# Two planes instead of four in a macaron block: pair merging on TensorE, and the shared expert's pieces spread out

## What is computed

```
x = x + 0.5 * ffn(layernorm(x))
x = x + linear_attention(layernorm(x))      # 16 heads, causal, b_qkv and b_out
x = x + 0.5 * ffn(layernorm(x))             # the same weights again

ffn(xf): scores = softmax(xf @ gate_w.T)                       # 64 experts
         idx    = top 6 of (scores + gate_b); weights = scores[idx]
         each expert takes its first CAP = 64 tokens, in token order; the others are dropped
         h = silu(xb @ w1[e].T) * (xb @ w3[e].T);  yb = h @ w2[e].T      # inner size 88
         y[token] += weight * yb
         z = silu(xf @ ws1.T) * (xf @ ws3.T) @ ws2.T                    # shared expert, inner 176
         return y + z
```

## Time and profile before

| | before |
|---|---|
| median of the runs | 537.15 us (536.43 to 538.29) |
| profiled execution | 532.9 us, span 531.2 us |
| mean granted TensorE clock | 0.793 of 2.4 GHz |
| busy, share of the span | PE 67%, PEld 50%, DVE 58%, ACT 39%, POOL 45% |
| HBM read and written | 39.53 MB and 31.46 MB |
| first slot loop and its adds | about 52 to 164 us |
| second slot loop and its adds | about 393 to 500 us |

### The profile page before, as it was taken

How to read it: one execution, slowest core, us unless ns; L and a number is a source line. 1 busy time by engine, 2 the same in 40 slices (tenths; PEclk the granted TensorE clock), 3 DMA queues, 4 the chain that set the end, 5 groups by cost and what they waited for, 6 DMA issues and landing times.

```text
span 531.2 us, 14693 instructions
## 1 busy us (share of the span) xinstructions
PE 356.6 (67%) x5808; PEld 263.3 (50%) x5812; DVE 307.6 (58%) x999; ACT 207.8 (39%) x543; POOL 237.0 (45%) x215
## 2 busy tenths in 40 slices
PE   0874589999960013598999999218848999998000
PEld 0851475666650012376788888118327667666000
DVE  6488363545430994454777775394985544545077
ACT  3983112322310067744677762169722232231000
POOL 7161747887872000403333333001537888887400
PEclk9987567999995556678999999657855699999555
DMA  8999961001015996000111111454200100100396
GB/s 272 369 268 341 318 185 15 5 11 14 5 6 218 407 401 239 2 2 2 40 40 40 40 40 49 109 218 139 61 8 8 12 11 6 17 5 6 108 426 257
DMA packets 49746, 62.64 MB, mean 118 GB/s; under 512 B 21701, under 2 KB 36248, under 8 KB 47183
## 3 DMA queue, kind: packets, MB, share of 16 engines
q1 hardware_dynamic: 37423, 60.51, 33.3%
q0 software_dynamic: 12288, 1.70, 3.2%
HBM read 39.53 MB, written 31.46 MB: 134 GB/s over the span
## 4 chain that ended last, share of the span: by engine, by line
PE 53%; DVE 23%; DMA 9%; ACT 6%; issue 5%; POOL 3%; SPq 1%; POOLq 0%; DVEq 0%; ACTq 0%
PE bank L769 6%; PE upper L864 5%; PE bank L705 5%; DVE X L957 5%; PE bank L718 5%; PE upper L705 4%; DMA Cb<-planes_d 4%; PE upper L778 3%; DVE Cb L1094 3%; DVE bn L962 3%; DVE Cb L1025 3%; POOL planes_d L452 3%; ACT Cb L560 2%; ACT A L508 2%; PE bank L880 2%
## 5 line engine op out<-in xcount | busy, mean ns | idle before, releaser
L452 POOL DMA_INDIRECT planes_d<-Bb,put_i x64 | 101.4, 1584 | 28.0 <-issue 14.8
L480 POOL TENSOR_TENSOR Bb<-Cb,chm 128x576 f32<-128x576 f32 x32 | 36.9, 1183 | 124.3 <-PE upper L909 69.6
L466 POOL DMA_INDIRECT A<-rows_d,tok_i x64 | 68.0, 1063 | 41.6 <-DVE put_i L1066 22.7
L672 PE MATMUL bank<-ident,A 128*128 128x128 f32 x96 | 21.3, 396 | 81.9 <-ACT A L508 65.1
L672 PEld LDWEIGHTS bank<-ident,A 128*128 128x128 f32 x96 | 17.0, 209 | 85.1 <-ACT A L508 52.3
L1106 DVE TENSOR_SCALAR Bb<-upper,A 64x128 f32<-64x128 f32 x128 | 44.4, 347 | 1.3
L1094 DVE TENSOR_TENSOR Cb<-Cb,upper 88x512 f32<-88x512 f32 x24 | 16.4, 683 | 44.8 <-ACT Cb L560 44.8
L769 PEld LDWEIGHTS bank<-ring,w1s 128*88 128x88 f32 x256 | 34.2, 191 | 8.0 <-issue 8.0
L433 POOL TENSOR_TENSOR Bb<-Eb,st 128x512 f32<-128x512 f32 x8 | 8.3, 1043 | 63.8 <-DVE st L1013 63.8
L560 ACT ACTIVATE Cb<-bank 88x512 f32<-88x512 f32 x24 | 14.2, 592 | 55.1 <-PE upper L705 55.1
L769 PE MATMUL bank<-ring,w3s 128*88 128x64 f32 x256 | 35.6, 270 | 0.0
(11 more groups left out here) (162 smaller groups left out, 804.7 us busy)
## 6 DMA issues: line engine op xcount, KB each, us to landing
planes_d<-zeros SPq DMA_DIRECT2D x8, 2048.0 KB, 15.9
rows_d<-A SPq DMA_DIRECT2D x8, 512.0 KB, 6.0
A<-planes_d SPq DMA_DIRECT2D x4, 1024.0 KB, 6.0
PL<-planes_d SPq DMA_DIRECT2D x4, 1024.0 KB, 10.0
Bb<-planes_d SPq DMA_DIRECT2D x4, 1024.0 KB, 13.7
Cb<-planes_d SPq DMA_DIRECT2D x4, 1024.0 KB, 18.0
w1s<-in_w1T SPq DMA_DIRECT2D x4, 704.0 KB
w3s<-in_w3T SPq DMA_DIRECT2D x4, 704.0 KB
```

Of the source, the lines that this page charges most:

```text
L452: pool.indirect_dma_start(out=planes_d[f], in_=Y[:, s, :], in_offset=None, out_offset=bass.IndirectOffsetOnAxis(ap=put_i[:, s:s + 1], axis=0),
L466: pool.indirect_dma_start(out=GAT[:, t % RING, :], out_offset=None, in_=rows_d, in_offset=bass.IndirectOffsetOnAxis(ap=tok_i[:, t:t + 1], ...
L480: pool.tensor_tensor(out=VX[:, :, :, c, :].rearrange("p q h f -> p (q h) f"), in0=VN.rearrange("p q h f -> p (q h) f"), in1=chm[:, c:c + 1 ...
L672: ins = pe.transpose(bank[g % 2][:, (i % 4) * P:(i % 4 + 1) * P], A[:, i, :], ident[:, :])
```

## The change

- Two planes instead of four, one for each slot parity. Where a token of a slot's second expert is also in its first, the second's row is added to the first's on chip: `spread` (DVE) writes the first expert's tokens as a diagonal for eight slots, `token_rows` (PE) turns it into a row on 64 partitions by a matmul with ones, `match` (DVE) compares it with the second expert's tokens. The result `SAME` is a 0/1 matrix of each slot. `merge` (PE) multiplies it with the second half of Y, `add_second` (DVE) adds that to the first half. The index of a merged row is put out of range, so that POOL's DMA leaves it out.
- The turn's order. PE: transpose, expert_out(s - 2), hidden(s - 1), merge(s - 2), then the piece. DVE: weigh, gate, add_second, then the rest. add(s) on POOL now waits for add_second.
- The shared expert's pieces. Groups 4 and 5 have their hidden pieces ahead of the loop; groups 0 to 3 have their pieces in turns 8, 10, ... 30; outputs of 4 and 5 in turns 32 and 33; groups 6 and 7 in turns 34 to 39, behind the loop. SP's read of the planes waits for six shared groups instead of eight; `update` still waits for all eight.
- The table and first comparison ahead. differences(2) and (3), the first token_rows, spread(0), match(0), table(2) and table(3) stand before the loop; the other three spreads and matches in turns 4 to 19.
- The planes are cleared ahead of everything in one go; the loads of experts 16 to 63 wait until the second slot has been transposed.
- The factor 0.5 moves from `weigh` into `update`, whose two adds become scalar_tensor_tensor.

```diff
+    SPREAD, ROW_TURN, MATCH = (4, 12, 18), (5, 13, 19), (6, 13, 19)
+    LOOPED = 4
+    TURNS = NS + 9
-        planes_d = [nc.dram_tensor(f"planes{f}_d", (4 * T, D), ...
+        planes_d = [nc.dram_tensor(f"planes{f}_d", (2 * T, D), ...
+        PLANES = (A_flat[:, 0:HP], A_flat[:, HP:T], PL[:, 0:HP], PL[:, HP:T])
         def shared_part(s):
+            if s < NS:
+                g, k = divmod((s - 8) // 2, 3)
+                return (g, k) if s >= 8 and s % 2 == 0 and g < LOOPED else None
+            if s < NS + EARLY:
+                return LOOPED + s - NS, 2
+            g, k = divmod(s - NS - EARLY, 3)
+            return (LOOPED + EARLY + g, k) if LOOPED + EARLY + g < NSH else None
 # SP
-                    clear_planes(sp, 0, (2, 3))
+                    sp.wait_ge(xbT_ps, 2)
                     for h in range(1, NQT):
                         load_experts(h)
...
-                sp.wait_ge(z_added, NSH * (f + 1))
+                sp.wait_ge(z_added, NSH * f + LOOPED + EARLY)
 # PE
+                def token_rows(h):
+                    pe.wait_ge(rows_set, NQT * f + h + 1)
+                    if NQT * f + h:
+                        pe.wait_ge(same_ready, NQT * f + h)
+                    ss = slice(QSL * h, QSL * h + QSL)
+                    pe.matmul(bank[LOOK[1]][CAP:P, :], ones[:, :], ROWS[:, ss, :].rearrange("p s c -> p (s c)"),
+                              start=True, stop=True).then_inc(rows_ps, 1)
...
+                differences(2)
+                differences(3)
+                token_rows(0)
...
+                def merge(s):
+                    if s % QSL == 0:
+                        pe.wait_ge(same_ready, NQT * f + s // QSL + 1)
+                    pe.wait_ge(weighed, f * NS + s + 1)
+                    pe.matmul(bank[(4, 7)[s % 2]][0:CAP, D:2 * D], SAME[:, s, :], Y[CAP:P, s, :], start=True, stop=True)\
+                        .then_inc(merged, 1)
...
+                for s in range(TURNS):
                     if s < NS:
                         xb_turn(s)
+                    if s == 2:
+                        pe.wait_ge(dr_sb, NQT * (f + 1))
+                    if 2 <= s < NS + 2:
+                        expert_out(s - 2)
                     if 1 <= s <= NS:
                         hidden(s - 1)
-                    if s >= 2:
-                        expert_out(s - 2)
+                    if 2 <= s < NS + 2:
+                        merge(s - 2)
+                    if s in ROW_TURN:
+                        token_rows(1 + ROW_TURN.index(s))
+                    if s < 2:
+                        look_up(2 + s)
 # DVE
                     dve.wait_ge(z_added, NSH * (n // 2 + 1))
-                    for k in range(4):
-                        then(dve.tensor_tensor(xt, xt, PLANES[g]...[:, :, k, :], ALU.add))
+                    for k in range(2):
+                        then(dve.scalar_tensor_tensor(xt, PLANES[g]...[:, :, k, :], 0.5, xt, ALU.mult, ALU.add))
...
+                def spread(h):
+                    ss = slice(QSL * h, QSL * h + QSL)
+                    dve.tensor_tensor(ROWS[:, ss, :], ident[0:CAP, 0:CAP].unsqueeze(1).broadcast_to([CAP, QSL, CAP]),
+                                      sl[0:CAP, 1, ss].unsqueeze(2).broadcast_to([CAP, QSL, CAP]), ALU.mult).then_inc(rows_set, 1)
+
+                def match(h):
+                    ss = slice(QSL * h, QSL * h + QSL)
+                    dve.wait_ge(rows_ps, NQT * f + h + 1)
+                    then(dve.tensor_tensor(SAME[:, ss, :], bank[LOOK[1]][CAP:P, :].rearrange("p (s c) -> p s c", s=QSL),
+                                           sl[CAP:P, 1, ss].unsqueeze(2).broadcast_to([CAP, QSL, CAP]), ALU.is_equal))
+                    then(dve.tensor_reduce(sl[CAP:P, 0, ss], SAME[:, ss, :], AX, ALU.max))
+                    then(dve.scalar_tensor_tensor(sl[CAP:P, 0, ss], sl[CAP:P, 0, ss], float(T), sl[CAP:P, 1, ss], ALU.mult, ALU.add))
+                    dve.scalar_tensor_tensor(put_i[CAP:P, ss], sl[CAP:P, 0, ss], 2.0, plane0[CAP:P, ss], ALU.mult, ALU.add)\
+                        .then_inc(same_ready, 1)
...
+                def add_second(s):
+                    dve.wait_ge(merged, f * NS + s + 1)
+                    dve.tensor_tensor(Y[0:CAP, s, :], bank[(4, 7)[s % 2]][0:CAP, D:2 * D], Y[0:CAP, s, :], ALU.add).then_inc(y_sb, 1)
+
+                for s in range(TURNS + 1):
+                    if 2 <= s < NS + 2:
+                        weigh(s - 2)
                     if 1 <= s <= NS:
                         gate(s - 1)
+                    if 2 <= s < NS + 2:
+                        add_second(s - 2)
+                    if s in (2, 3):
+                        slots(s)
+                    elif s in SPREAD:
+                        spread(1 + SPREAD.index(s))
...
+                    part = shared_part(s - 1)
+                    if part and part[1] < 2:
+                        shared_gate(*part)
+                    elif part:
+                        shared_add(part[0])
+                    if s in MATCH:
+                        match(1 + MATCH.index(s))
```

More of the change, by code:

```diff
@@ L81, in macaron_kernel @@
         rows_d = nc.dram_tensor("rows_d", (T, RWD), F32, kind="Internal").ap()
-        planes_d = [nc.dram_tensor(f"planes{f}_d", (4 * T, D), F32, kind="Internal").ap() for f in range(2)]
+        planes_d = [nc.dram_tensor(f"planes{f}_d", (2 * T, D), F32, kind="Internal").ap() for f in range(2)]
         attn_d = nc.dram_tensor("attn_d", (T, D), F32, kind="Internal").ap()
@@ L110, in macaron_kernel @@
         plane0 = sb("plane0", [P, NS])
+        ones = sb("ones", [CAP, CAP])
         gate_s = sb("gate_s", [P, NE])
@@ L274, in shared_part, with clear_planes @@
         def shared_part(s):
-            if s >= NS:
-                return NSH - EARLY + s - NS, 2
-            g, k = divmod(s - 8, 4)
-            return (g, k) if 0 <= g < NSH - EARLY and k < 3 else None
+            if s < NS:
[5 more added lines that the diff above has]
+            return (LOOPED + EARLY + g, k) if LOOPED + EARLY + g < NSH else None
         def early(g):
-            return g >= NSH - EARLY
+            return LOOPED <= g < LOOPED + EARLY
         def hidden_order(f, g, k):
-            return f * 2 * NSH + (2 * (g - NSH + EARLY) if early(g) else 2 * (EARLY + g)) + k
+            n = g - LOOPED if early(g) else EARLY + g if g < LOOPED else g
+            return f * 2 * NSH + 2 * n + k
         block = ctx.enter_context(nc.Block())
-        def clear_planes(queue, f, parts=range(4)):
-            for k in parts:
+        def clear_planes(queue, f):
+            for k in range(2):
                 dst = planes_d[f][k * T:(k + 1) * T, :].rearrange("(p a i) d -> p a (i d)", p=P, i=4)
@@ L422, in _ @@
                 count(c_of_p[k * CAP:(k + 1) * CAP, :], 0, [[0, 1]], 1)
-                count(plane0[k * CAP:(k + 1) * CAP, :], k, [[0, NS // 2], [2, 2]], 0)
+                count(plane0[k * CAP:(k + 1) * CAP, :], 0, [[0, NS // 2], [1, 2]], 0)
+            then(pool.memset(ones[:, :], 1.0))
             pool.iota(slot_ce[:, :, :], pattern=[[1, CAP], [0, NE]], base=0, channel_multiplier=0,
@@ L551, in copy_differences @@
                                    ACT.Copy).then_inc(dr_sb, 1)
-                for h in range(2):
+                for h in range(NQT):
                     copy_differences(h)
@@ L572, in silu @@
                     act.activation(SG[s % 2], bank[2 + s % 2][0:I, 0:P], ACT.Silu).then_inc(silu_done, 1)
-                for s in range(NS + 2):
+                for s in range(TURNS):
                     if s < NS:
@@ L736, in look_up @@
                         pe.wait_ge(tokens_ready, NQT * f + h - 1)
+                    if h == 3:
+                        pe.wait_ge(same_ready, NQT * f + 1)
                     for j in range(HE):
@@ L741, in look_up @@
                     ins.then_inc(look_ps, 1)
-                for g in range(NSH - EARLY, NSH):
+                def token_rows(h):
[5 more added lines that the diff above has]
+                              start=True, stop=True).then_inc(rows_ps, 1)
+                for g in range(LOOPED, LOOPED + EARLY):
                     for k in range(2):
@@ L955, in update @@
                     dve.wait_ge(part_in[g], 16 + 32 * (1 + n // 2))
-                    for k in range(4):
-                        then(dve.tensor_tensor(xt, xt, PLANES[g].rearrange("p (i k d) -> p i k d", i=GI, k=4)[:, :, k, :], ALU.add))
+                    for k in range(2):
+                        then(dve.scalar_tensor_tensor(xt, PLANES[g].rearrange("p (i k d) -> p i k d", i=GI, k=2)[:, :, k, :], 0.5,
+                                                      xt, ALU.mult, ALU.add))
                     dve.memset(st[:, 0, 0:1], 0.0).then_inc(group_ready, 1)
@@ L1076, in ffn @@
                 slots(1)
+                spread(0)
+                match(0)
                 table(2)
+                table(3)
                 def gate(s):
```

74 lines of the change are left out of this document (34 added, 40 removed).

## The result

| | before | after |
|---|---|---|
| median of the runs | 536.79 us (534.69 to 538.29, 4 runs) | 569.81 us (569.59 to 576.26, 4 runs) |
| profiled execution: time, span | 532.9, 531.2 us | 569.59, 567.8 us |
| granted clock over the span | 0.793 | 0.786 |

The ratio is 1.0675, with a 95% interval of 1.062 to 1.0731: **slower by 33 us**, where 15 were forecast. On the profiled executions the difference is 36.7 us. Timed from the first gather of each stage (52.06 and 407.12 now; 52.11 and 393.32 before), it is 13.8 us by the start of stage 2 and 22.8 us in stage 2.

What follows compares the result with a forecast made beforehand. POOL was taken to bound the loop, with PE ending it after the change. Stage 1 +2.2 and stage 2 +6.4 gave +8.6, plus 6 for the clock: +14.6 on the median 537.15, say 552 us; 8-in-10 range 536 to 572.

Steps and rivals of the forecast that it cites:

- Part 1, two planes: Reads and updates of X: second read falls from 23.2 to 11.6 us, adds halve; 9 us saved counted in stage 1.
- Part 2, the start: Start of stage 2's loop: spread, broadcast and match ahead of slot 0 make POOL's first add 2.2 us late, at 409.7.
- Part 3, the turn: Loop turns on PE: cycle expert_out, weigh, merge makes a pair 5.4 us; POOL's last add at 501.9 instead of 497.00.
- Seven turns at 2.16: Loop's first turns at 1.2 GHz: with slots(3), spread, match and a first piece, they bring slot 7 to 432.9.
- two more broadcasts with their comparisons: Loop from slot 7 to turn 31: 2 us on top of 59.4 us for 11 pairs.
- Part 4, behind the loop: Groups 6 and 7 after the loop: 9.5 us each, 19.0 for both, then X updates ending at 534.4 instead of 528.0.
- The clock: PE's granted clock falling in new gaps of loop and tail: 3 us a stage, 6 in all, ends none and 14.
- low clock: Rival, chance 0.18: clock falls in most gaps, slowing pieces behind the loop by 11 us a stage and some inside; 578 us.
- The pieces stay hidden: Rival on the faster side, chance 0.14: weigh or merge cost PE nothing, only gathers hold it, pairs about 5.0; 519 us.
- (4): Sign in the changed kernel's trace: two adds a group and reads of half the length.
- (5): Sign in the changed kernel's trace: granted clock mostly 1.0 in the loop.
- The port pair: SBUF ports shared by VectorE and GpSimd: each spread could hold POOL back half a microsecond; 0 to 2 us a stage.

Runs made afterwards that it cites:

- fillers: Changed kernel plus one idle 512-column PE matmul, its result unread, ahead of each shared piece from turn 33 on: 564.33 us, ratio 1.0561 to the kernel before.
- the two fastest versions: Changed kernel, merge one turn later, with more PSUM banks and reordered pieces behind the loop: 528.76 us; or pieces and their VectorE part as before the change: 525.62 us.
- undoing a half of such a pair: Changed kernel, pieces back at their earlier places but VectorE's part still one iteration later: 626.0 us; with the merge also one turn later, 629.78 us.
- the version with the lowest median: Changed kernel with merge one turn later, pieces at the places of the kernel before and VectorE's part in the piece's own iteration: 525.62 us, ratio 0.9825.

## Why the prediction was wrong, step by step

The sign, the engine that takes over and the shape of the end were right; the size was less than half of it. Forecast: +14.6. Measured on the profiled executions: +36.7.

**Part 1, two planes.** Right, and better than counted. The first adds into X start together with the last shared add, so no read shows. From the first add to the next stage's first gather it is 208.24 us (198.88 to 407.12) and was 221.57: 13.3 saved, 9 counted. The scalar_tensor_tensor took 1.24 and 1.23, the value taken.

**Part 2, the start.** Right: first add 17.0 us behind the first gather (407.12 to 424.12), 16.4 by my sum (409.7 against 393.32).

**Part 3, the turn: this is the step that failed, in three terms.**

1. *"Now it has a cycle through VectorE: expert_out [...], weigh [...], merge"* and *"add_second is off this path."* This is the step that failed first. The path is a longer one: `hidden`, silu, gating product, `add_second`, the piece's part on VectorE, weighing, merge, piece. In the pair shown above `hidden` has 0.78 us of it, silu 0.28, gating product 0.28, `add_second` 0.20, the shared add 0.38 and weighing 0.70. A pair takes 5.7 and not 5.4 (504.13 to 509.80), some 3 us over 11 pairs. That it comes so near is luck: I counted two merges at 0.19 and two weighings on a path of two turns, where there is one merge, and left out silu, gating product and `hidden`. The merge's own term was too small as well: *"one of expert_out's two matmuls is 0.19 [...] I take that, bounds 0 and 0.44."* It measured 0.40 to 0.43 at full clock, at the upper bound, and 0.61 at 1.2 GHz.
2. *"Seven turns at 2.16."* I added the merge to the full-clock turns and not to these. At 1.2 GHz a turn takes 3.01 (hidden 1.37, merge 0.61, transpose 0.40, second product 0.63). Slot 7 was added at 450.04, 42.9 us behind the first gather, 3.3 later than forecast; the other 2.7 of these seven turns I can't place (the 3.9 that I had put between them for the comparison may have lain beside them in part).
3. *"[...] two more broadcasts with their comparisons: 59.4 + 2"*. I had charged the broadcasts to PE and not asked who is queued behind the comparison on VectorE. It is the weighing, and PE waits for the weighing: 1.5 us of idle PE and a piece at 3.2 to 3.5 instead of 1.9. In stage 2 the two places make four pairs of 7.79, 7.30, 7.79 and 7.35 us, 7.4 more than four of 5.7, where 2 was counted. Turn 31 begins some 9 us late in all, of which 3.3 was there at slot 7; the comparisons taken out gave back 17 us over both stages.

Stage 2 behind its first gather is 16.4 us longer than the sum without its clock term: 9.3 up to turn 31, 1.7 in turns 31 to 33 and 5.4 behind them; the clock term covered 3. The run with the merge one turn later takes away most of what the merge waits for (13.7 us of waits become 0.9) and is 18 us faster. I had written "Now it has a cycle through VectorE" and costed the merge's work in it, but never asked what the same work costs where it waits for nothing. That question would have shown the term. A slip besides: 409.7 + 22.7 is 432.4 and not 432.9, so the sum is half a microsecond too long in each stage.

**Part 4, behind the loop.** 19.0 us for both groups, measured 24.4 in either stage, 5.4 more: three of the four hidden pieces take 2.0 + 1.5 to 1.7 us instead of 1.0 + 0.9, at a granted clock of 0.71. That the excess is clock is shown: with fillers the clock is 1.00 and a group takes 9.56, my 9.5. What I took for given was the chain itself (piece, silu, product, piece), and more banks with another order of the pieces shorten it by 9 us.

**The clock.** 3 us a stage was the term; behind the loop alone it was 5, and two of three comparisons in the loop each made a piece slow besides. The rival "low clock" (578) was nearer in time than the forecast, but its mechanism holds for a part only: the windows of the loop after turn 8 have 0.88 to 1.00, and fillers behind the loop brought 5.5 us.

**The faster side.** "The pieces stay hidden" had its switch at the pair: 5.0 us and below. It was 5.7. The late merge makes that rival come true in substance: PE then isn't held by VectorE, and with more banks the kernel is 5.6 us *faster* than with four planes (528.76 against 534.33). The price of 519 that I gave to this rival is within 10 us of the two fastest versions.

**What was to show it.** (1) Pairs of 5.4: 5.7, with the weighing ending just before each merge, as said. (2) POOL idle between its last adds: yes, this is its timeline in the kernel after, where the earlier trace rows have gaps of 0.3:

```profile
520.27 1.55 POOL L472 DMA_INDIRECT planes_d<-Bb,put_i  x1 [2.18 <-DVE Bb L1177]
...
525.90 1.55 POOL L472 DMA_INDIRECT planes_d<-Bb,put_i  x1 [1.73 <-DVE Bb L1177]
```

(3) The first adds wait for the last shared add: yes, but at 198.9 and 554.4 and not near 183 and 524. (4) Yes. (5) Mostly, from the eighth turn on.

**The port pair.** It stood for up to 2 us a stage. POOL's gathers took 1082 ns on average from 412 to 528, against 1.0 to 1.06 in the earlier trace rows, so at 29 of them it is 1 us at most. One spread a stage shows it: of the four, the one of turn 4 starts just ahead of a gather, and that gather is half a microsecond longer (timelines of DVE and POOL in the kernel after; in stage 1 it is 1.53 us at 74.25). The others fall beside an add or begin when a gather is under way, and these have their usual length. So the spreads cost POOL 0.5 us a stage and not 2.

```profile
429.23 0.67 DVE L1115 TENSOR_TENSOR Eb<-ident,sl 64x512 f32<-64x512 f32 x1
429.31 1.52 POOL L486 DMA_INDIRECT A<-rows_d,tok_i  x1 [0.30 <-issue]
```

## What to carry to other kernels

When work is put into a loop behind a wait on another engine, cost the *wait*, which is all that this engine has queued ahead of the awaited instruction, and not only the work; then ask whether the step can run one turn later, where the result is there already. A move of work between places has to be judged together with the order on the engines that finish it: undoing a half of such a pair cost more here than the change did. And a part that is hidden while another engine is the bound (pieces behind the loop, 7 us) can cost several times as much (up to 26 us) once that engine no longer is.

## What was unexpected of the hardware

- One merge (64 x 64 weights, 128 columns, two records) takes 0.36 us even where nothing waits, 0.40 to 0.43 right behind a wait, and 0.61 at 1.2 GHz; the two products of expert_out, with 88 rows, take 0.37 together. So the wait in front of it exposes only 0.04 to 0.07 of it. Half of expert_out's time was never the price of one product: in the groups by line of the kernel after its 256 records last 341 ns on average and fill 32.8 us, so they lie largely over one another, while the 128 records of the merge last 326 ns and fill 30.9 us. The kernel has the two products write different halves of the partitions (`bank[CAP * k:CAP * k + CAP]`), while a merge stands alone; whether that is why they overlap wasn't tested.
- PE busy by the profile without a gap, and the clock stayed low: this window of the kernel after has PE busy 16.00 of 16.00 us at a granted clock of 0.50; it reads 0.60 in the next 16 us, where the first shared piece lies, and 0.93 in the 16 after.

```profile
64.00:80.00 16.00, 16.00 (x87) 10.08 (x87) 10.12 (x32) 2.56 (x10) 7.34 (x6) 0.50 0.96 291
```

- Half the planes didn't make the adding loop shorter: POOL's slot of add and gather costs 3.24 us where nothing waits in the version with the lowest median too (1.59 + 0.30 + 1.04 + 0.31), and its last add starts 117 us behind the first gather, where it was 104 and 110 before. From the first add into X to the next first gather it is 209.3 us instead of 221.6, and there it gains.
